# One product for B and C in a Mamba and soft-MoE layer kernel, and a new order of its visits

## The reference, cut to what matters

```python
h = layernorm(x) * (1 + ca) + sa
xn = h * rsqrt(mean(h * h) + eps) * norm_w           # 128 channels
z, x_ssm, Bm, Cm, dt_raw = split(xn @ in_proj_w.T)   # 256, 256, 128, 128, 4 columns
xh = silu(causal_conv4(x_ssm) + conv_b)              # 4 heads of 64
dt = softplus(dt_raw + dt_bias); dA = exp(-exp(A_log) * dt)
# scan over tokens: state = state * dA + dt * xh * Bm; y = state . Cm
y = (y + D * xh) * silu(z)
x = x + ga * (h + y @ out_proj_w.T)
h = layernorm(x) * (1 + cb) + sb
xn2 = unit_rows(h) * norm_gamma                      # soft mixture of experts
logits = xn2 . unit_rows(slot_embeds)                # 8 experts x 64 slots
slots = dispatch_softmax(over tokens... of logits) applied to xn2
out = x + gb * (combine_softmax(logits) applied to w2(gelu(w1(slots) + b1)) + b2)
```

## Time and profile before

| | |
|---|---|
| runs | 229.61, 230.07, 230.66 us; median 230.07 |
| profiled execution | its own time 228.26 us, its span 226.3 us |
| granted clock of TensorE | 1.0 throughout, the 2.4 GHz level |
| busy share | TensorE 91%, VectorE 61%, ScalarE 53%, GpSimd 26% |
| setup, until about 16 us | mostly DMA and transposes |
| pass 0 | about 16 to 83 us |
| pass 1 | about 83 to 151 us |
| experts and combination | from 151 us to the end |

### The profile page before, as it was taken

One profiled execution on the slowest core, in us unless ns is written; L12 is line 12 of the kernel. 1 busy time (PEld: TensorE's weight loads), 2 busy tenths in 40 slices (PEclk: granted clock), 3 DMA queues, 4 the chain that ended last, 5 costly groups with the idle time before them and its releaser, 6 DMA issues.

```text
span 226.3 us, 4248 instructions
## 1 busy us (share of the span) xinstructions
PE 206.5 (91%) x1575; PEld 149.1 (66%) x1575; DVE 137.8 (61%) x372; ACT 120.1 (53%) x264; POOL 59.9 (26%) x147
## 2 busy tenths in 40 slices
PE   3779999996799999999996799989999999999993
PEld 2546476674477795565674486774956849569993
DVE  3698859998999857859998865530220402204662
ACT  3688996532479756895523576658145081450000
POOL 6553884026524203983025500000000000000000
PEclk9999999999999999999999999999999999999999
DMA  6404002000500000002400000014133041300122
GB/s 192 116 0 141 6 5 75 20 3 16 202 15 3 0 3 0 1 2 66 125 0 1 0 3 0 3 52 133 49 93 96 1 138 49 93 3 3 58 70 61
DMA packets 15345, 10.73 MB, mean 47 GB/s; under 512 B 1773, under 2 KB 13654, under 8 KB 15326
## 3 DMA queue, kind: packets, MB, share of 16 engines
q1 hardware_dynamic: 15100, 10.31, 15.2%
q10 hardware_dynamic: 226, 0.16, 0.3%
HBM read 9.34 MB, written 1.07 MB: 46 GB/s over the span
## 4 chain that ended last, share of the span: by engine, by line
PE 63%; DVE 20%; ACT 6%; issue 4%; POOL 2%; DMA 2%; ACTq 1%; DVEq 0%; POOLq 0%
PE bank L577 28%; PE bank L922 13%; PE bank L904 11%; DVE seg_m L1370 5%; PE bank L814 2%; DVE bst L1183 2%; DVE hh L1246 2%; DVE cshift L1407 2%; DMA vec_nat<-ffn_slot_norm_gamma_dram 2%; PE bank L829 2%; DVE hh L1238 2%; DVE x1tok L1388 1%; DVE xhT L1379 1%; PE bank L761 1%; PE bank L835 1%
## 5 line engine op out<-in xcount | busy, mean ns | idle before, releaser
L1444 DVE TENSOR_TENSOR eo<-bank,seg_e 128x512 f32<-128x512 f32 x8 | 5.5, 692 | 47.9 <-PE bank L922 47.9
L922 PEld LDWEIGHTS bank<-w_sb,zsT 128*64 128x64 f32 x256 | 27.8, 137 | 3.0 <-issue 3.0
L922 PE MATMUL bank<-w_sb,xcT 128*64 128x128 f32 x256 | 28.8, 273 | 0.0
L922 PE MATMUL bank<-w_sb,zsT 128*64 128x128 f32 x256 | 28.8, 273 | 0.0
L922 PEld LDWEIGHTS bank<-w_sb,xcT 128*64 128x64 f32 x256 | 27.8, 137 | 0.0
L904 PE MATMUL bank<-slotsT,w_sb 128*128 128x512 f32 (+1 forms) x64 | 26.1, 558 | 0.2 <-ACT zsT L1140 0.2
L1140 ACT ACTIVATE zsT<-bank,vecT 128x512 f32<-128x512 f32 x16 | 10.7, 687 | 24.9 <-PE bank L904 24.9
L577 PE MATMUL bank<-xnT,winT 128*128 128x512 f32 x48 | 22.4, 603 | 0.0
L490 POOL TENSOR_TENSOR root<-root,neg_half 128x2 f32<-128x2 f32 (+1 forms) x24 | 20.2, 843 | 2.0
L1306 DVE SCALAR_TENSOR_TENSOR xcT<-bank,convw,xcT 128x510 f32<-128x510 f32 (+2 forms) x24 | 17.3, 736 | 4.5 <-ACT xcT L1050 4.2
L904 PEld LDWEIGHTS bank<-slotsT,w_sb 128*128 128x128 f32 x64 | 11.4, 190 | 12.6 <-issue 12.1
(11 more groups left out here) (165 smaller groups left out, 412.9 us busy)
## 6 DMA issues: line engine op xcount, KB each, us to landing
w_sb<-in_L_ffn_w_dram SPq DMA_DIRECT2D x16, 256.0 KB, 2.8
mods_bc<-mod_dram SPq DMA_DIRECT2D x4, 320.0 KB, 3.4
xin<-in_L_attn_x_dram SPq DMA_DIRECT2D x4, 256.0 KB, 2.8
out_dram<-x1tok SPq DMA_DIRECT2D x16, 64.0 KB, 1.5
mods_bc<-mod_dram SPq DMA_DIRECT2D x4, 192.0 KB, 3.1
seg_e<-mod_dram SPq DMA_DIRECT2D x1, 512.0 KB, 3.9
eo<-in_L_attn_in_proj_w_dram SPq DMA_DIRECT2D x1, 384.0 KB, 3.9
eo<-in_L_wmod_dram SPq DMA_DIRECT2D x1, 256.0 KB, 4.4
```

The source lines that it names most:

```text
L922: q = nc.tensor.matmul(o[j * S:(j + 1) * S, tile_cols(b)], act_h[j][k // 2][:, k % 2, at:at + S], w2_sb[j][:, k, :], start=k == 0 and b == ...
L1444: V.tensor_tensor(o, bank[4 + 2 * (it % 2) + g][:, :].rearrange("p (b d) -> p b d", d=P), b2_bc[:, it, :].unsqueeze(1).broadcast_to((P, 4, ...
```

## The change

**B and C.** The scores are Bm_s . Cm_t = xn_s' (Wb' Wc) xn_t, with Wb and Wc the two 128x128 blocks of the weights. The setup now multiplies Wb' Wc once, in place of transposing both blocks; every pair makes U = (Wb' Wc)' xn where it made B, and the scores multiply UT with xnT itself. The C product and `copy_c` are gone. The dt weights stay a block of four columns. norm_w is applied once by `scale_win` and once more by the scale of `copy_u`. xn2T gets its own memory.

**Split visits.** `add_basis` becomes `gated_h` and `add_x` for each half, `gate_weights`, `scores`, `t_xh`, `dt_times_x`, `copy_scores` and `first_tap` are visits for each half or block, `y_of` loses its diagonal product to `d_times_x` and waits for each weighed tile by itself, `statistics2` and `centre2` are two visits, `t_logits` goes by token tile, `shifts` and `exps` each become two, `norm_slots` and `fill_slots` go by pair of slot blocks. `project_out` waits for gated weights alone, no longer for the basis.

**New turns.** All five engines have new tables.

```diff
-    Z0, X0, B0, C0 = 0, DI, 2 * DI, 2 * DI + P
+    Z0, X0, U0, DTC = 0, DI, 2 * DI, 2 * DI + P
+    B_BLOCK, C_BLOCK = 2 * DI // P, 2 * DI // P + 1
...
-            pipeline(sp, [((2, 4, 1, 5), next_x), ((7, 6, 8, 9), next_mods), ((0, 3, 10, 11), send_parts)])
+            pipeline(sp, [((2, 4, 1, 5), next_x), ((8, 6, 9, 7), next_mods), ((0, 3, 10, 11), send_parts)])
...
-            def add_basis(j, it):
-
-                wait(pool, h_done, j, it)
-                wait(pool, mods_in, j, it)
-                for bi in range(BP):
-                    t = slice(bi * NT, (bi + 1) * NT)
-                    q = nc.gpsimd.tensor_tensor(basis[j][:, t, :], hh[j][:, t, :],
-                                                mods_bc[j][:, bi, 2, :].unsqueeze(1).broadcast_to((P, NT, P)), ALU.mult)
-                q.then_inc(pool_own[1][j], 1)
-                wait(pool, pool_own, j, it, POOL_BASIS)
-                nc.gpsimd.tensor_tensor(basis[j][:, :, :], basis[j][:, :, :], xin[j][:, :, :], ALU.add
-                                        ).then_inc(basis_done[1][j], 1)
+            def gated_h(bi):
+                def visit(j, it):
+                    wait(pool, h_done, j, it, (bi + 1) * NT)
+                    wait(pool, mods_in, j, it)
+                    nc.gpsimd.tensor_tensor(basis[j][:, of_batch(bi), :], hh[j][:, of_batch(bi), :],
+                                            mods_bc[j][:, bi, 2, :].unsqueeze(1).broadcast_to((P, NT, P)), ALU.mult
+                                            ).then_inc(basis_own[1][j], 1)
+                return visit
+
+            def add_x(bi):
+                def visit(j, it):
+                    wait(pool, basis_own, j, it, bi + 1)
+                    nc.gpsimd.tensor_tensor(basis[j][:, of_batch(bi), :], basis[j][:, of_batch(bi), :],
+                                            xin[j][:, of_batch(bi), :], ALU.add).then_inc(basis_done[1][j], 1)
+                return visit
 
             variances = lambda j: mv[j][:, :, 1]
             mean_squares = lambda j: ms[j][:, :]
-            def gate_weights(j, it):
-
-                if it == 0:
-                    pool.wait_ge(s_act0, ACT_WO)
-                wait_before(pool, o_ps, j, it)
-                for bi in range(BP):
-                    q = nc.gpsimd.tensor_tensor(wo_gated[j][:, bi, :, :], woT[:, :, :],
-                                                mods_bc[j][:, bi, 2, :].unsqueeze(1).broadcast_to((P, CT, P)), ALU.mult)
-                q.then_inc(basis_done[1][j], 1)
+            def gate_weights(bi):
+                def visit(j, it):
+                    if it == 0:
+                        pool.wait_ge(s_act0, ACT_WO)
+                    wait(pool, mods_in, j, it)
+                    wait_before(pool, o_ps, j, it)
+                    nc.gpsimd.tensor_tensor(wo_gated[j][:, bi, :, :], woT[:, :, :],
+                                            mods_bc[j][:, bi, 2, :].unsqueeze(1).broadcast_to((P, CT, P)), ALU.mult
+                                            ).then_inc(gated_done[1][j], 1)
+                return visit
 
...
-            visits = [((0, 1, 19, 21), var_root1), ((2, 4, 20, 22), ms_root1), ((5, 7, 23, 26), softplus),
...
+            visits = [((0, 2, 27, 28), var_root1), ((1, 4, 30, 29), ms_root1), ((5, 9, 31, 36), softplus),
...
-            for n in range(ROW_BLOCKS):
-                q = nc.tensor.transpose(bank[1 + n // 4][:, tile_cols(n % 4)], w_nat[:, n, :], ident[:, :])
+            for n in range(2 * CT):
+                nc.tensor.transpose(bank[1][:, tile_cols(n)], w_nat[:, n, :], ident[:, :])
+            mm(bank[2][:, 0:P], w_nat[:, B_BLOCK, :], w_nat[:, C_BLOCK, :])
             pe.wait_ge(s_dt, 16)
-            nc.tensor.transpose(bank[2][:, 2 * P:2 * P + H], dt_nat[:, :], ident[0:H, 0:H]).then_inc(s_pe0, 1)
...
                     pe.wait_ge(s_act0, (ACT_WIN, ACT_SN)[j])
                 for t in range(TP):
-                    q = mm(b3[:, t * H:(t + 1) * H], xnT[j][:, tile_cols(t)], winT[:, DT0:ROWS])
+                    q = mm(b3[:, t * H:(t + 1) * H], xnT[j][:, tile_cols(t)], winT[:, DTC:DTC + H])
                 q.then_inc(proj_ps[1][j], 1)
 
                 wait_before(pe, slots_done, j, it)
                 mm(b0[:, :], winT[:, X0:X0 + P], xnT[j][:, :]).then_inc(proj_ps[1][j], 1)
                 mm(b1[:, :], winT[:, X0 + P:X0 + 2 * P], xnT[j][:, :]).then_inc(proj_ps[1][j], 1)
                 wait_before(pe, slotsT_done, j, it)
-                mm(b2[:, :], winT[:, B0:B0 + P], xnT[j][:, :]).then_inc(proj_ps[1][j], 1)
+                mm(b2[:, :], winT[:, U0:U0 + P], xnT[j][:, :]).then_inc(proj_ps[1][j], 1)
 
             def project2(j, it):
 
+                wait(pe, xbu_done, j, it, 3)
+                mm(bank[4 * j + 2][:, :], winT[:, Z0:Z0 + P], xnT[j][:, :]).then_inc(z_ps[1][j], 1)
+
+            def project3(j, it):
                 wait(pe, nabs_done, j, it)
-                mm(bank[4 * j + 3][:, :], winT[:, C0:C0 + P], xnT[j][:, :]).then_inc(proj_ps[1][j], 1)
-                wait(pe, xbc_done, j, it, 3)
-                mm(bank[4 * j + 2][:, :], winT[:, Z0:Z0 + P], xnT[j][:, :]).then_inc(z_ps[1][j], 1)
-
-            def project3(j, it):
-                wait(pe, xbc_done, j, it, 4)
                 mm(bank[4 * j + 3][:, :], winT[:, Z0 + P:Z0 + 2 * P], xnT[j][:, :]).then_inc(z_ps[1][j], 1)
 
-            def scores(j, it):
-
-                wait(pe, xbc_done, j, it)
-                for bi in range(BP):
+            def scores(bi):
+                def visit(j, it):
+                    wait(pe, xbu_done, j, it)
                     wait(pe, conv_done, j, it, bi + 1)
                     o = bank[4 * j + bi]
                     t0 = bi * L
-                    mm(o[:, 0:L], BT[j][:, t0:t0 + P], CTr[j][:, t0:t0 + L])
-                    mm(o[:, L:L + P], BT[j][:, t0 + P:t0 + L], CTr[j][:, t0 + P:t0 + L]).then_inc(g_ps[1][j], 1)
+                    mm(o[:, 0:L], UT[j][:, t0:t0 + P], xnT[j][:, t0:t0 + L])
+                    mm(o[:, L:L + P], UT[j][:, t0 + P:t0 + L], xnT[j][:, t0 + P:t0 + L]).then_inc(g_ps[1][j], 1)
+                return visit
 
...
-            def y_of(bi):
-                def visit(j, it):
-
+            def d_times_x(bi):
+                def visit(j, it):
                     wait(pe, dtx_done, j, it, bi + 1)
                     if it == 0:
                         pe.wait_ge(s_act0, ACT_SMALL)
@@ -750,9 +756,16 @@
                         nc.tensor.matmul(bank[4 * j + bi][:, k * L:(k + 1) * L], diag_d[:, k, :],
                                          xhT[j][:, k, bi * L:(bi + 1) * L], start=k == 0, stop=False,
                                          skip_group_check=True)
-                    wait(pe, m_done, j, it, 3 * bi + 3)
+                return visit
+
+            def y_of(bi):
+                def visit(j, it):
                     for g in range(NT):
                         for h in range(H):
+                            if g == 0 and h % 2 == 0:
+                                wait(pe, m_done, j, it, 3 * bi + h // 2 + 1)
+                            elif h == 0:
+                                wait(pe, m_done, j, it, 3 * bi + 3)
                             o = bank[4 * j + bi][(h % 2) * HD:(h % 2 + 1) * HD, (h // 2) * L:(h // 2 + 1) * L]
                             if g == 0:
                                 s = seg_m[j][:, h // 2, (h % 2) * L:(h % 2 + 1) * L]
...
-                    wait(pe, basis_done, j, it)
+                    wait(pe, gated_done, j, it, bi + 1)
...
+                    for n, m in ((0, 0), (0, 1), (1, 0), (1, 1), (0, 2), (0, 3), (1, 2), (1, 3)):
+                        wait(pe, disp_done, j, it, 2 * bi + n + 1 if m < 2 else 2 * bi + 2)
                         o = by_token(j, bi, m // 2)[:, (m % 2) * (P + 1):(m % 2 + 1) * (P + 1)]
-                        for n in range(NT):
-                            q = mm(o, e_disp[j][:, n, tile_cols(m)], xn2tok[j][:, bi * NT + n, :],
-                                   start=n == 0, stop=n == NT - 1)
-                        if m % 2:
+                        q = nc.tensor.matmul(o, e_disp[j][:, n, tile_cols(m)], xn2tok[j][:, bi * NT + n, :],
...
                 return visit
 
-            def first_tap(j, it):
-                for k in range(CT):
+            def first_tap(k):
+                def visit(j, it):
                     wait(act, proj_ps, j, it, k + 2)
                     A(xcT[j][:, k, :], bank[4 * j + k][:, :], ACT.Identity, bias=vecT[:, RCB + k:RCB + k + 1],
-                      scale=convw[:, k, TAPS - 1:TAPS]).then_inc(xbc_done[1][j], 1)
+                      scale=convw[:, k, TAPS - 1:TAPS]).then_inc(xbu_done[1][j], 1)
+                return visit
+
+            def copy_u(j, it):
                 wait(act, proj_ps, j, it, 4)
-                A(BT[j][:, :], bank[4 * j + 2][:, :], ACT.Copy).then_inc(xbc_done[1][j], 1)
```

(29 more changed lines are left out.)

173 lines of the change are left out of this document (95 added, 78 removed).

## The result

The changed kernel takes 222.12 us (median of 4 runs, 221.62 to 224.42) against 229.97 for the kernel before; the ratio is 0.9675, 95% interval 0.9601 to 0.9748. That is a gain of 7.85 us where 4.1 were forecast: right in sign, outside the range. Measured again (e1), it had 223.32 us and a ratio of 0.9777 (0.9678 to 0.9875), a gain of 6.8 us.

The account below looks back on a forecast made before the run. The prediction saw no single engine as the bound, but a chain across TensorE, VectorE and ScalarE. Its terms 0.9 + 0.6 + 0.4 + 0.6 + 1.6 = 4.1 us, from 230.07, gave 226.0 us, range 223.2 to 228.9.

Parts of the forecast that it names:

- C: Weighs: VectorE waits behind GpSimd, 1.4 us a pass beyond the 0.3 taken, giving 227.8 us; chance 0.10.
- Rival D: Second buffer's segments wait for their rows' DMA, holding TensorE and VectorE; slower, 232.0 us at 3 us each; chance 0.10.
- But little of TensorE's share is on the path: Projection stages: of 3.5 us TensorE work removed little counts; only buffer 1's copy to CTr, 0.49 us each pass.
- term 1: Up to the first weigh of pass 0: 0.9 us gained, from the copy and new turns; bounds 0.3 and 1.3.
- term 4: Pass 1 up to its first weigh: 0.6 us, of which the copy 0.49; bounds 0.3 and 1.2.
- rival A: Whole kernel: only the cut copies return, new turns cost what they save; 1.4 us, 228.7; chance 0.20.
- so I take zero: Setup: one product replaces two transposes and the weight copy narrows; no gain, with 0.3 either way.
- Zero, with -0.5 to +0.5: Stretch from about 62 to 83 us: the change only re-cuts equal work, so no gain.
- term 3: Pass boundary: buffer 1's transposes come behind buffer 0's first products of pass 1; 0.4 us.
- terms 1, 2 and 5: Pass 0 to first weigh 0.9 us, pass 0 decay stage 0.6, pass 1 decay stage and norms 1.6.
- Rival B: Whole kernel: everything fits, decay stages at their upper bounds; gain 6.1 us, 224.0; chance 0.10.
- Term 2: Decay stage of pass 0: dt product moved ahead, y starts on its first tile; 0.6 us, bounds 0 and 1.3.

Follow-up runs that it names:

- e6: Changed kernel with the turns from the decays to the second norm's rows in the old order on all engines; 225.87 us, ratio 0.9872.
- e12: Changed kernel plus a filler: 5 TensorE products nobody reads, in the setup's idle stretch; 222.05 us, ratio 0.9699, profiled span 219.6.
- e10: Changed kernel with the product of the combined weights (U) issued twice in each half of each pass; 228.95 us, ratio 0.9951.
- e15: Kernel before with the product of B issued twice in each half of each pass; 232.19 us, ratio 1.015.
- e17: Changed kernel with the first z product issued twice in each half of each pass; 228.63 us, ratio 0.9945.
- e2: Kernel before with the product of the B and C weights alone, old visits and old turns; 229.79 us, ratio 1.0023.
- e5: Changed kernel's splits and new turns, but B and C multiplied apart, with the copies of C at later turns; 230.87 us, ratio 1.0081.
- e14: Changed kernel with VectorE's first nine and GpSimd's first five turns (setup) in the old order; 224.05 us, ratio 0.9766.
- e16: Changed kernel with one TensorE exchange undone: pass 1's second-half row transposes again ahead of the first half's first products; 222.23 us, ratio 0.974.
- e18: Changed kernel with y again waiting for all three weighed tiles of its half before its first product; 225.63 us, ratio 0.984.
- e8: Changed kernel with 11 TensorE products nobody reads added where TensorE idles in the setup; 223.79 us, ratio 0.98.

## Why the prediction was wrong

**What held.** The sign, and roughly the places, all somewhat earlier than forecast: the first decay of pass 0 at 33.70 and first weigh at 34.84 (forecast 34.4 and 35 to 35.4), the first gate at 37.71 (38.3), the first products of pass 1 at 80.47 (81 to 81.7), the first decay of pass 1 at 99.19 (about 100.2). SP's loads of x and of the modulation rows show no wait, as forecast.

**The rivals.** C's mechanism is real, and only its price is out. By the Trainium skill, "SBUF — State Buffer", section "Who interferes with whom", a VectorE instruction with two SBUF inputs and a GpSimd one that reads SBUF exclude one another for a whole instruction. The traces agree. Here are a gated-weights product and the weigh after it in e6, then such a product in e12:

```profile
34.47 1.19 POOL L526 TENSOR_TENSOR eo<-woT,mods_bc 128x256 f32<-128x256 f32 x1
34.98 1.21 DVE L1450 TENSOR_TENSOR seg_m<-seg_e,gm 128x512 f32<-128x512 f32 x1
```

```profile
99.92 1.18 POOL L526 TENSOR_TENSOR eo<-woT,mods_bc 128x256 f32<-128x256 f32 x1
```

Alone they take 0.72 and 0.68 us. In e6 the product starts 0.10 us after a weigh and waits for it, and the next weigh waits for the product. In e12 GpSimd pays, beside the weigh at 99.82, which keeps its 0.69; in pass 0 the first weigh of the three at 34.84 meets the last 0.32 us of a product and takes 0.87. Its 0.19 us more is the sign that the forecast named for C (over 0.7), far from the 1.1 and 0.7 us of C's sum, since the new turns leave few weighs beside GpSimd. The row at 103.34, from which the forecast concluded that the full price isn't borne out, met only the last 0.24 us of a product, and so could not tell. (C's own words also give 1.3 us for pass 1, not 0.7: 228.4 instead of 227.8.) What GpSimd takes from VectorE sits in the small steps of Q, 0.65 instead of 0.17 us each, before and after the change.

Rival D is out: the second half's first segments show no wait. But its sign, over 0.5 us for this DMA, came at another place: in e12's pass 0 the first half's segments wait 1.11 us, against 0.45 in the earlier trace rows, and the chain of work runs through it.

**First failed step: the base.** "The base is the profiled execution: ... its own time 228.26, which lies 1.81 below the median of 230.07; I subtract the sum from the median." The 1.81 us were taken as a constant. They are mostly falls of the clock, which the profiled execution happened not to have (its granted clock is 1.00 in every window of the earlier trace rows) and 90 of 103 executions of this kernel had. With the change they were rarer, and about 2.2 of the 7.85 us are that. By the 5.6 us at a full clock the forecast's own subtraction would have given 224.5, inside its range; so it is this step that took the measurement out of it.

**Second: "But little of TensorE's share is on the path."** It was argued from who waits for the convolution. The chain of the kernel before said otherwise: it runs through TensorE's projections without a gap from 20.05 to 29.48 us and from 87.50 to 92.70, and in pass 0 it goes from there over Q and the sums to the weigh, never through ScalarE, where term 1 placed its 0.49. e10, e15 and e17 show that what is added to TensorE there costs 4.4 to 5.7 us for 3.5, in either order. Removing it without new turns gives nothing clear (e2), because in pass 1 GpSimd's softplus was only 0.2 us ahead of TensorE. That wait is in no term: the forecast weighed GpSimd's roots and what it takes from VectorE, but not its softplus. And the sum is of product and turns as if each had a price of its own; e2 to e5 show that neither has a clear one without the other. The 0.49 us of each copy, which terms 1 and 4 and rival A booked as a gain by itself, isn't one by itself either, and the copy of U, taken as free, takes 0.68 us in e2 against 0.60 for B's.

**Third: two stages at zero, one too small.** The setup was costed for its products alone ("so I take zero"); VectorE's turns there put the first half's modulation ahead of the second half's statistics and free the rows of the modulation 0.75 us earlier in the profiles (0.4 to 1.0 by e14, within the spread). From the second norm to the hidden layer in pass 1 nothing was booked; it gave 1.07. The middle, "Zero, with -0.5 to +0.5" beside term 3's 0.4, gave 1.32: this stretch shrank by over 1 us, which the forecast had itself named as a sign of being wrong. e16 fits the 0.4. Against these, terms 1, 2 and 5 were too large by 0.35, 0.26 and 0.42. The balance is 5.77 - 4.1 = 1.7 us too little. Rival B's 6.1 us (which counts term 4 with 0.7 where the term has 0.6) is nearer to the 5.6 at a full clock, but by luck: it has other sizes in other stages.

Term 2's own step, y on its first tile, is right and under-priced in what hangs on it: 2.2 us for both passes by e18, where the forecast gave y's early start at most 0.8 in each.

**Open.** Why the falls near 58 and 125 us come in some executions and not in others with the same waits: e8 and the changed kernel have the same four idle stretches on TensorE ahead of 58 us (0.45, 0.82, 0.35 and 0.47 us), and only e8's clock falls. What the order of the decay stage is worth at a full clock. And whether the old order with the gated weights moved behind the second softplus, and nothing else, would let the product alone pay.

## What to carry to other kernels

Compare executions at the same granted clock before pricing a change, and ask whether the change moves idle stretches of TensorE: here 2.2 us of 7.85 came from the clock and not from the order of the work. In a kernel whose engines run fixed lists, work taken off one of them can be worth nothing while another engine's list ends at the same time, and turns moved without it may be worth nothing either; so look, at each place where engines meet, how far the second latest is behind the latest (here 0.2 us); forecast both together, stage by stage, and leave no stage at zero whose rows move. Where a small chain crosses two engines once for each half, look at which half's step stands behind which on the shared engine, and at what GpSimd does beside the small VectorE steps: that is what multiplies a delay.

## What the runs showed of the hardware

TensorE's granted clock fell to half (0.53 and 0.50 in windows of 4 and 2 us, the 1.2 GHz level) after TensorE had idled for about 2 us in the setup, though it had been busy for all of the 2 us before that, and stayed there for some 7 us of full work; 2.8 us were lost. With the filler in that place (1.22 us idle are left in e12's profile) the mean clock was 0.999 or 1.0 in six of six executions, without it in six of ten. The same program shows the fall in some executions and not in others, so one profile doesn't tell its rate. The Trainium skill, "TensorE: Matmul & The Clock Gate", section "What's actually happening", says that the point at which the clock changes varies from run to run; the runs here show that whether it falls at all varies too.

VectorE and GpSimd held each other up by whole instructions. Steps of 16 elements that read SBUF alone took 0.65 to 0.72 us beside GpSimd's products of 0.72 and 0.17 to 0.21 without them; a weigh that met a product from near its start took 1.21 instead of 0.68, and a product that came 0.1 us after a weigh 1.18 instead of 0.72. VectorE's products with an input in PSUM kept 0.68 beside GpSimd (the dt products at 97.84 in e12), and the small steps that read PSUM their 0.17.
